# ScalarE asks for its exponential-and-tanh table right behind the reciprocal sums of each pair of heads

## The reference

```
s   = clip(hs @ Ws1.T @ Ws2.T + bs2, -32, 32)        # per head 64 slots
z   = cumlogsumexp(s, over tokens)
es  = exp(s);  enz = exp(-z)
A   = tril(rope(q) @ rope(k).T) * 128**-0.5
qv  = softmax(enz * (A @ es), over slots)
W2  = tril((qv * enz) @ es.T)
o   = W2 @ v
o_g = rmsnorm(o) * g_norm * (g * sigmoid(g))         # g = hs @ Wg.T
x   = x + o_g @ Wo.T
```

## Time and profile before

| | |
|---|---|
| time, median of 3 runs | 626.18 us (625.65 to 626.44) |
| the profiled execution's own time | 624.78 us |
| its span | 623.0 us |
| TensorE matmuls busy | 583.9 us, 94% |
| weight loads busy | 498.4 us, 80% |
| VectorE busy | 483.1 us, 78% |
| ScalarE busy | 381.1 us, 61% |
| GpSimd busy | 283.7 us, 46% |

### The profile page before, as it was taken

The page is one execution under the profiler, slowest core; times in us unless marked ns, Lnnn a source line. Parts: engine busy times, 40 slices in busy tenths (PEclk is TensorE's granted clock), DMA queues, the critical chain, the costliest instruction groups (busy, mean ns, idle before and its releaser), DMA issues. The chain is left out here.

```text
span 623.0 us, 14116 instructions
## 1 busy us (share of the span) xinstructions
PE 583.9 (94%) x4426; PEld 498.4 (80%) x4426; DVE 483.1 (78%) x1118; ACT 381.1 (61%) x1182; POOL 283.7 (46%) x325
## 2 busy tenths in 40 slices
PE   5999999999999999999999999887779999999997
PEld 5878888888888888988988888775558878877776
DVE  6999878887887886976976987667567777886765
ACT  4177755755856756657567476656676666567362
POOL 3557644754754664663754664456641202111000
PEclk9999999999999999999999999998799999999999
DMA  8202000200200200200200000700000000000000
GB/s 268 69 0 65 22 2 1 86 0 0 84 0 0 84 0 0 84 0 0 82 3 1 17 3 1 269 4 1 3 3 9 3 13 11 2 11 11 3 11 17
DMA packets 10321, 19.35 MB, mean 31 GB/s; under 512 B 2336, under 2 KB 5920, under 8 KB 10144
## 3 DMA queue, kind: packets, MB, share of 16 engines
q1 hardware_dynamic: 10272, 18.74, 9.0%
HBM read 17.55 MB, written 1.05 MB: 30 GB/s over the span
## 5 line engine op out<-in xcount | busy, mean ns | idle before, releaser
L842 ACT ACTIVATE sa_v<-bank 128x256 f32<-128x256 f32 x64 | 24.5, 383 | 55.5 <-PE bank L250 55.3
L914 POOL TENSOR_TENSOR sa_qe<-sa_ex,sa_enz 128x256 f32<-128x256 f32 x32 | 23.3, 729 | 74.7 <-ACT sa_ex L816 74.7
L816 ACT ACTIVATE sa_ex<-sa_okb,sa_minus_top 128x64 f32<-128x64 f32 x128 | 42.9, 339 | 22.7 <-DVE sa_minus_top L711 22.6
L908 POOL TENSOR_TENSOR sa_qt<-sa_rope_cos,sa_rope_sin 128x512 f32<-128x512 f32 x32 | 41.2, 1287 | 30.9 <-DVE sa_rope_sin L757 29.7
L248 PE MATMUL bank<-ht_hi,sa_qk_hi 128*128 128x512 f32 x128 | 54.6, 427 | 0.2 <-DVE sa_rope_sin L757 0.2
L248 PE MATMUL bank<-sa_vg_hi,ht_hi 128*128 128x512 f32 x128 | 52.8, 413 | 1.3 <-DVE sa_gate L762 1.3
L250 PE MATMUL bank<-sa_vg_hi,ht_lo 128*128 128x512 f32 x128 | 50.6, 395 | 0.0
L250 PE MATMUL bank<-ht_hi,sa_qk_lo 128*128 128x512 f32 x128 | 50.5, 395 | 0.0
L249 PE MATMUL bank<-sa_vg_lo,ht_hi 128*128 128x512 f32 x128 | 50.5, 395 | 0.0
L249 PE MATMUL bank<-ht_lo,sa_qk_hi 128*128 128x512 f32 x128 | 50.2, 392 | 0.0
L755 DVE TENSOR_TENSOR sa_rope_cos<-bank,con 128x512 f32<-128x512 f32 x64 | 43.8, 685 | 7.4 <-PE bank L250 7.3
(11 more groups left out here) (210 smaller groups left out, 1846.0 us busy)
## 6 DMA issues: line engine op xcount, KB each, us to landing
sa_qk_raw<-in_wqk SPq DMA_DIRECT2D x8, 512.0 KB, 5.0
sa_vg_raw<-in_wvg SPq DMA_DIRECT2D x8, 512.0 KB, 3.3
sa_wo_raw<-in_wo SPq DMA_DIRECT2D x8, 256.0 KB, 3.5
xf_w_raw<-in_w SPq DMA_DIRECT2D x2, 640.0 KB, 10.7
xf_w_raw<-in_w SPq DMA_DIRECT2D x1, 1152.0 KB, 9.7
xs<-in_x SPq DMA_DIRECT2D x2, 512.0 KB, 4.6
hn<-in_w SPq DMA_DIRECT2D x2, 512.0 KB, 4.9
out<-xs SPq DMA_DIRECT2D x8, 128.0 KB, 1.7
```

Of the source, the lines that this page charges most:

```text
L816: ins = act.activation(ex[:, s, u, :], okb[:, s, u, :], ACT.Exp, bias=minus_top[:, s, u:u + 1], accum_out=total[:, g, u:u + 1])
L908: pool.tensor_tensor(dst[:, h, c * HALF:(c + 1) * HALF], rope_cos[:, s, :], rope_sin[:, s, :], ALU.add).then_inc(roped, 1)
```

## The change

Behind the second `enz` exponential of each pair (step CS 1) ScalarE asks for the set `exp_and_others`, which holds exponential and hyperbolic tangent. `n` is a plain number at build time, so that the request stands once in each pair: eight times in all, of them one in the prologue between CS 1 and T 1 of pair 0, six at the end of pair 0 and of the loop's turns, and one at the end of pair 6, ahead of the last pair.

```
--- before.py
+++ after.py
@@ -874,6 +874,8 @@
                         act.wait_ge(qe_done, at(i, 2 * n + 1))
                     act.activation(enz[:, 4 * n:4 * n + 4, :], log_cs[:, n, :].rearrange("p (b m) -> p b m", b=4),
                                    ACT.Exp, scale=-1.0).then_inc(enz_done, 1)
+                    if n == 1:
+                        act.preload_act_table_set("exp_and_others")
 
         return every_turn(act, H_ACT, run, banks, {"RS": lambda: rotary.scalar(act)})
 
```

## The result

The changed kernel takes 618.11 us in the median of 4 runs (617.53 to 618.72), the kernel before 625.96 beside it (625.65 to 626.44): a ratio of 0.9878, with a 95% interval of 0.9866 to 0.9891, so 7.85 us less, and between 6.8 and 8.4 by the interval. The forecast was 619.8. The profiled execution of the changed kernel took 618.72, its span 616.9. Lines behind 877 have numbers two higher than before (L1613 is L1615, L914 is L916), and the new request is L878.

The account below looks back on a forecast made before the run. TensorE, busy 94%, was taken as the bound, paused by ScalarE's late table loads. Gains of 5.0 + 0.93 + 0.45 = 6.4, less 0 for the new places, gave 619.8 us from a median of 626.18; range 618.0 to 624.0.

Parts of the forecast that it names:

- Count: Table loads on ScalarE: eight added behind the second `enz` exponentials, the eight automatic ones at L845 and L1613 gone.
- Price of one load: On ScalarE: 1.30 to 1.40 us where a load is taken out, 1.30 where it is put in.
- New places, 0: Behind `enz` in prologue, turns and ahead of the last pair: idle time or other pauses cover the load, cost 0.
- Pairs 1 to 6, 0.84 each: Main term: TensorE's pause ahead of transposes T 3 goes almost whole, 6 × 0.84 = 5.0 us.
- The list of signs: What the changed profile would show, among it E 1 on TensorE still released by the mask with 0.6.
- Pair 0, 0.93: VG 1 on TensorE waits 0.93 for VectorE's gate, which waits for the tangent; that pause goes.
- Feed-forward, 0.45: VectorE's wait of 0.47 for the first feed-forward tangent: gain between 0 and 1.4, taken as 0.45.
- A: Rival: VectorE sets the pace behind T 3, half the main term is lost, about 622.3 us; chance 0.11.
- B: Rival: a load at the new place takes 2.57, costing 6.4 together, so 626.2 us; chance 0.04.
- C: Rival: an automatic load returns at E 0 each pair, 9.1 lost, 2.7 slower, 628.9 us; chance 0.05.
- D: Rival: the automatic loads at L845 stay, the added ones are covered, 626.2 us; chance 0.03.
- E: TensorE's granted clock: its low stretch could fall on other matmuls, give or take 1 to 2 us; no chance given.

Follow-up runs that it names:

- experiment 2: The changed kernel with a second, unneeded table load (sigmoid set) ahead of each added one: 626.07 us, ratio 0.9993 to the kernel before.
- experiment 3: The changed kernel with eight further loads requested where the automatic ones had stood, sixteen in place of eight: 626.62 us, ratio 1.0015 to the kernel before.
- experiment 5: The kernel before with the request only for the tangents of pairs 1 to 6, end of pair 0 included: 620.09 us, ratio 0.9918.
- experiment 6: The kernel before with the request only in the prologue, for pair 0's tangent: 624.29 us, ratio 0.998.
- experiment 7: The kernel before with the request only behind pair 6, for the feed-forward part's first tangent: 624.92 us, ratio 0.999.
- experiment 1: The changed kernel, unaltered, measured and profiled again: 617.66 us, ratio 0.9877 to the kernel before.
- experiment 8: The changed kernel with the copy of T 3 ahead of SN 0's exponentials on ScalarE: 618.24 us, ratio 0.9882 to the kernel before.
- experiment 4: The kernel before with the request only in the loop's turns, for the tangents of pairs 2 to 6: 626.23 us, ratio 0.9989.
- experiment 9: The changed kernel with T 3's copy ahead of SN 0 on ScalarE and O 1 ahead of QK 5 on VectorE: 617.79 us, ratio 0.9874 to the kernel before.

## Why the prediction was right

**Count.** As forecast: eight loads at the new line, eight at L794, none at the old places (the prediction's sixteen leave out the three at L367, L778 and L859, which the change doesn't touch). The automatic placing respects a set that the code asks for.

**Price of one load.** 1.30 at the old place; 1.29 where a second is put behind the first (experiment 2). By the prediction's estimate from the figure of the Trainium skill (ScalarE: Activation LUTs, What ACT_TABLE_LOAD costs), 2.66 us a switch, the change would have given about nothing. No run here shows a drain beside the load: in each row read the load starts 0.01 or 0.02 behind the end of the activation or load ahead, and what follows starts 0.01 or 0.02 behind the load.

**New places, 0.** Right: 0.12 or less for all of them up to the last pair (experiment 3, within what two executions of one kernel differ). The cover shrank as worked out, in the turns from 1.81 to 0.50 of ScalarE's idle time, in the last pair from 0.80 to 0.46 of TensorE's. Experiment 2 shows what lies behind it: one further load at each place costs 5.3, and 1.6 by the clock in that trace.

**Pairs 1 to 6, 0.84 each.** 0.87 each, 5.23 in all against 5.0 (5.26 alone, experiment 5). The pause of T 3 went whole and QK 5 followed without one: of the 0.02 to 0.07 by which the bank was to fit, 0.06 is seen. What I called the upper bound is passed by 0.03 a turn, and I can't place that. The pause of E 1 at the turn's end shrank by 0.2, from 0.61 to 0.41, but this is no part of the gain: it is SN 0, whose weight loads start 0.2 late behind W2P, as worked out (0.38 of cover left). Experiment 3, with T 3's pause back, has 0.39 to 0.42 there too, in pairs 2 to 5. The list of signs said 0.6 for this pause, against the prediction's own working.

**Pair 0, 0.93.** 1.14 (1.12 alone, experiment 6). Besides the pause of VG 1, the step behind it, QK 5, had waited 0.15 for its bank in the kernel before, which the prediction overlooked: 0.93 + 0.15 = 1.08. The last 0.06 is open.

**Feed-forward, 0.45.** 1.37 (experiment 7): the term that was mis-sized, at the upper end of the bounds that I gave, 0 to 1.4. I had taken VectorE's wait of 0.47 as the whole effect. Behind it VectorE has no idle time, but it isn't of constant length. The timeline of VectorE and GpSimd in the kernel before, and then in the changed one:

```profile
457.78 1.28 POOL L1680 TENSOR_TENSOR xf_w_lo<-xf_w_raw,xf_w_hi 128x512 fp32r<-128x512 f32 x1 [2.80 <-ACT xf_w_hi L1640]
...
457.85 1.23 DVE L1513 SCALAR_TENSOR_TENSOR xf_half_scale<-xf_rank,xf_score 128x8 f32<-128x8 f32 x1
```

```profile
451.70 1.33 POOL L1682 TENSOR_TENSOR xf_w_lo<-xf_w_raw,xf_w_hi 128x512 fp32r<-128x512 f32 x1 [1.39 <-ACT xf_w_hi L1642]
...
452.77 0.28 DVE L1515 SCALAR_TENSOR_TENSOR xf_half_scale<-xf_rank,xf_score 128x8 f32<-128x8 f32 x1
```

The comparison of ranks works on eight elements a partition and takes 0.28 after, 1.23 before. In the kernel before it starts 0.07 behind GpSimd's product of 512 elements and ends with it, at 457.85 + 1.23 = 459.08 against 457.78 + 1.28 = 459.06. Counted from the score matmuls, the load held back ScalarE's `w_hi`, and so GpSimd's product, by 1.4, and VectorE's comparison by 0.4 only, and the two met. After, the comparison begins when the product is nearly over, and still ends with it (453.05 and 453.03). Experiments 1, 2, 7 and 8, without a load there, have 0.28 or 0.29; experiments 3 to 6, with one, have 1.23. So 0.47 of wait and 0.95 of a stretched instruction, 1.42, of which 1.37 arrives: the matmuls at 460.65 wait for VectorE's rotary product (L1451), which ends at 460.50. That the load sets this meeting is shown by the runs. The next row of VectorE in the kernel before ends with GpSimd's next product in the same way (459.78, and 459.02 + 0.74 = 459.76):

```profile
459.12 0.66 DVE L1515 SCALAR_TENSOR_TENSOR xf_half_scale<-xf_half_scale 128x8 f32<-128x8 f32 x1
```

In the seven later sequences both of VectorE's instructions take 0.17. That GpSimd holds VectorE by a common way to the memory is read from the ends that coincide, and wasn't tried by itself. The Trainium skill (SBUF — State Buffer, SBUF: two separate sides) says that VectorE and GpSimd share a pair of ports, and that, where VectorE's instruction has two inputs in SBUF and GpSimd's reads SBUF, the one that comes second waits for a whole instruction of the other; that agrees with these rows.

**The rivals.** A (half of the main term) didn't come about: the pause went whole. VectorE is next, though, as experiments 8 and 9 show, 0.2 to 0.3 behind. B's cause isn't there, and its price, tried with a second load, is 5.3 and not 6.4. C appears as soon as the tables at the loop's head differ (experiment 4), at another place and for less, 0.76 a turn. D is excluded by the groups. E: the stretch at 406 cost 1.66 in one of the profiled executions, and not in its repetition; it is chance, of the size that I allowed. (The prediction calls TensorE little busy in the low stretch of the earlier trace rows; the row has 2.77 of 4.00.)

**The sum.** 7.7 instead of 6.4, of which 0.91 is the feed-forward term (1.36 in the whole change), 0.21 pair 0 and 0.23 the pairs between. The forecast of 619.8 less these 1.3 is 618.5, against 618.1 measured.

## What to carry to other kernels

A table load costs its 1.3 us only where its engine is behind; ask for the set at a place where the engine is going to idle, and read beforehand how long the idle time ahead of the next wait is, since one load fitted here and two didn't. Where it doesn't fit and TensorE stops for it, look at the clock behind the stop too (1.6 us a time went there in experiments 2 and 4). Ask for it on every way into a loop, or an automatic load comes back at its head. When a delay is taken out, look also at what ran beside the delayed work: two of the three terms were larger than their wait, one by a bank and one by a VectorE instruction that no longer met GpSimd's.

## What was not expected of the hardware

A VectorE instruction on 128x8 took 1.23 us where it began beside a GpSimd product of 128x512, 0.28 where it met only the product's end, and 0.17 where it met none; a pause isn't the only form in which a wait shows, a long duration is another. And the granted clock fell from 1.00 to 0.50 for some 3 us at 406 in one execution and stayed at 1.00 in another of the same program, behind the same stretch of little TensorE work (0.32 of 2.00 busy in both): 1.66 us of difference between two profiles that no edit made. In the loop the clock fell in two traces alone, once in experiment 2 and twice in experiment 4, each time behind a turn's head where TensorE stood still for W2P for some 1.4 us; at the seven other such heads of these traces it stayed at 1.00.
